# A two-layer graph kernel: output scaled by one VectorE instruction and added by GpSimd, probabilities' residual on VectorE, adjacency two graphs ahead, other orders at both ends

## The chip, the cores and the metric

The kernel runs on one core of a Trainium2 chip. The metric is the device time in microseconds of one execution, median over several. The engines named here are TensorE (PE, with its weight loads PEld), VectorE (DVE), ScalarE (ACT), GpSimd (POOL) and SyncE (SP), whose queue issues nearly all DMA transfers. They run side by side and wait for one another through semaphores only; each takes its own instructions strictly in order.

## The reference

`x` has 128 graphs of 128 nodes with 512 features, `adj` is one 128x128 matrix shared by all of them. Cut to what is computed:

```python
# layer 0
h = jnp.maximum(_layernorm(x), 0.0)
A = jnp.einsum('od,bdn->bon', adj, h)             # W1 = W2 = adj
C = A + b[None, :, None]
pre = A[:, :, None, :] + (C - A)[:, :, :, None]
x = x + jnp.max(jax.nn.relu(pre), axis=-1)
# layer 1
h = jnp.maximum(_layernorm(x), 0.0)
q, k, v = (h @ Wq + bq), (h @ Wk + bk), (h @ Wv + bv)    # 8 heads of 64
scores = einsum('bihd,bjhd->bhij', q, k) / 8 + mask(adj == 0)
x = x + einsum('bhij,bjhd->bihd', softmax(scores), v)
```

The kernel uses that layer 0 adds one number per node: the row's largest entry of `A` plus the bias, through a relu. A number that is the same for a whole row leaves the layer norm of layer 1 unchanged, so one normalised `h` serves both layers.

## The kernel before

One graph is one tile of 128 rows and 512 columns. Every matrix product is made of three fp16 products: each operand is split in a head (fp16 of the value) and a residual (fp16 of what the head leaves out), and head x head, head x residual and residual x head are summed in PSUM. So nearly every operand costs two instructions on ScalarE, VectorE or GpSimd: one for the head, one for the residual.

The work on the 128 graphs is a software pipeline written out by hand. Each engine has a function `slot(base, k)`, run for k = 0 to 127, and what it does in slot k belongs to graphs at fixed distances: x loaded 7 ahead (`LOAD_AHEAD`), statistics 6 ahead, normalised `h` 5 ahead, transposed `h` 5 ahead, adjacency product 4 ahead (`PREP_AHEAD`), its row maximum 3 ahead (`AMAX_AHEAD`); scores, softmax and value rows 5 behind, probabilities times values 6 behind, output 7 behind.

In slot k TensorE runs: `scores` of graph k-5 (24 matmuls), two `qk_chunk`s (12 matmuls each; a chunk is 128 columns of Wq or Wk for a group of four graphs, so eight chunks make a group), `adjacency` of graph k+4 (3 matmuls), `v_rows` of k-5 (12 matmuls), `probs_times_v` of k-6 (24 matmuls). ScalarE writes the heads, the two exponentials of each softmax (a head in fp16, a copy in fp32) and `x1`, the input plus layer 0's number. VectorE runs `adjacency_out` (the row maximum), `v_rest`, `softmax_shift` (`masked`, `row_max`, `shifted`), `attention_out` and the statistics. GpSimd computes the norm's scales and the residuals of `h`, of q/k (`qk_rest`) and of the probabilities (`probs_rest`), and adds the value bias to `x1` (`add_bv`). SyncE issues load, transpose of `h`, store and transpose of the probabilities, in that order in each slot.

PSUM has eight banks: two of `proj` for q/k chunks, `proj` bank 2 (`A_BANK`) for the adjacency product, `proj` bank 3 (`V_BANK`) for value rows, two of `sc` for scores, two of `o_ps` for the output. `adjacency(k)` waits until VectorE has taken the row maximum of graph k-1 out of `A_BANK` (`a_evac`), `v_rows` until `v_rest` of the graph before has emptied `V_BANK` (`v_evac`), `probs_times_v` until `attention_out` of the graph before has emptied `o_ps` (`y_done`).

Ahead of slot 0 stands a prologue. The weights come as fp32 and are scaled by a power of two that follows from their largest entry. For each of the four matrices VectorE finds the peak, TensorE brings it to all rows (`peak_to_rows`, o_ps<-ident,peak), VectorE makes the scale (`scales_of`), ScalarE writes the heads (`w_head`), VectorE the residuals (`w_rest`). The first four graphs are transposed on TensorE (`turn`) and copied out (`turn_out`), and their adjacency products go to four different banks (`FIRST_BANKS`). Slots 0 to 4 have orders of their own on GpSimd and ScalarE (`early_slot`). Behind slot 127 stands a tail of five graphs (`TAIL`), whose scores alternate between the banks of `sc` and of the q/k chunks.

Of the kernel before, what the change touches and what calls it, by code (L numbers as in the profile page):

```python
# [24 lines left out]
LOAD_AHEAD, MOMENTS_AHEAD, NORM_AHEAD, TURN_AHEAD, PREP_AHEAD, AMAX_AHEAD = 7, 6, 5, 5, 4, 3  # L25
ATTN_BEHIND, OUT_BEHIND, STORE_BEHIND = 5, 6, 7
V_BEHIND, V_OUT_BEHIND, Y_BEHIND, BV_BEHIND = 5, 6, 7, 4
HT_GROUPS = 3
DVE_RESTS = 3


def graph_layers(nc, x, adj, b0, wq, bq, wk, bk, wv, bv, out):
# [6 lines left out]
    with ExitStack() as ctx:  # L39
# [131 lines left out]
        def _(sp):  # L171
            def load(base, k):
                if in_range(base, k):

                    wait(sp, xc_done, base + k - RING + 1)
                    sp.dma_start(x_in[:, k % RING, :], x[base + k, :, :]).then_inc(x_loaded[k % RING], 16)

            def store(base, k):
                if in_range(base, k):
                    sp.wait_ge(y_done, base + k + 1)  # L180
                    sp.dma_start(out[base + k, :, :], y[:, k % 2, :]).then_inc(y_stored[k % 2], 16)
# [3 lines left out]
            for k in range(1, PREP_AHEAD):  # L185
                load(0, k)
# [25 lines left out]
            def slot(base, k):  # L212
                load(base, k + LOAD_AHEAD)
# [8 lines left out]
            for i in range(ATTN_BEHIND):  # L222
                transpose_probs(B, i - ATTN_BEHIND)
                if i != 2:
                    store(B, i - STORE_BEHIND - (i > 2))
            for k in range(-3, 0):
                store(B, k)
            for k in range(2):
                sp.wait_ge(y_stored[k], 16 * (B // 2))

        @block.gpsimd
        def _(pool):
# [48 lines left out]

            def qk_rest(base, k, u):
# [22 lines left out]
            pool.wait_ge(bias_loaded, 64)  # L305
            assert (NORM_AHEAD, MOMENTS_AHEAD) == (5, 6)

            def early_slot(base, k):
# [4 lines left out]
                rest(base, k + NORM_AHEAD)  # L313
                qk_rest(base, k, u + 1)
                norm_scales(base, k + MOMENTS_AHEAD)
                add_bv(base, k - BV_BEHIND)

            def slot(base, k):
# [4 lines left out]
                probs_rest(base, k - ATTN_BEHIND)  # L323
# [7 lines left out]
            for k in range(-BV_BEHIND, 0):  # L331
                add_bv(B, k)
            for graph in TAIL:
                probs_rest(*graph)

        @block.scalar
        def _(act):
            def normalise(base, k):

                if in_range(base, k):  # L340
# [496 lines left out]
```

## Time and profile before

| | |
|---|---|
| median of 3 runs | 1345.38 us (1343.56 to 1346.32) |
| the profiled execution, its own time | 1345.62 us |
| its span, first to last instruction | 1343.7 us |
| TensorE busy, share of the span | 1298.3 us, 97% |
| VectorE | 1076.1 us, 80% |
| ScalarE | 946.6 us, 70% |
| GpSimd | 1107.3 us, 82% |
| mean granted TensorE clock | 0.990 |

The span is 1.92 us shorter than the execution's own time. Busy shares are means over the whole span. The rows further down split the span in stretches: the start up to about 62 us, the steady part, and the tail behind the last slot, from 1292.68 us on.

### The profile page before, as it was taken

To read this page: it belongs to the slowest core of one execution; us is meant where nothing else is said; L and a number is where in the kernel's file an instruction comes from. 1 tells how busy PE (TensorE), PEld (TensorE's weight loads), DVE (VectorE), ACT (ScalarE), POOL (GpSimd) and SP (SyncE) were. 2 spreads that over 40 slices of the span, in tenths; PEclk is the share of its full clock that TensorE was granted. 3 is DMA by queue.
4 is the path that set the end of the run, shared out by engine and by line. 5 is a ranking of instruction groups with operands and counts; after the bars stand their busy time and mean duration, and the time that the engine had idled before them with its cause. 6 is when DMAs were issued, how large, how long until landed. Compare 5 with 4: busy or idle time off the path is not lost.

```text
span 1343.7 us, 30432 instructions
## 1 busy us (share of the span) xinstructions
PE 1298.3 (97%) x11177; PEld 681.4 (51%) x11177; DVE 1076.1 (80%) x2235; ACT 946.6 (70%) x1425; POOL 1107.3 (82%) x1160
## 2 busy tenths in 40 slices
PE   5899999999999999999999999999999999999984
PEld 2355555555555555555555555555555555555542
DVE  6678888888888878878878888888888888888677
ACT  5787777776776776776776777777777767767542
POOL 4589988988888888888888888888888888888662
PEclk9999999999999999999999999999999999999987
DMA  6345555555555655655555546545555555455424
GB/s 180 68 113 129 142 134 119 141 135 122 139 133 126 139 130 130 137 128 133 137 125 142 134 119 143 133 119 146 130 122 146 127 125 143 127 127 126 94 73 110
DMA packets 437316, 172.19 MB, mean 128 GB/s; under 512 B 402608, under 2 KB 402736, under 8 KB 437168
## 3 DMA queue, kind: packets, MB, share of 16 engines
q1 hardware_dynamic: 435824, 169.98, 53.0%
q8 instruction: 89, 1.46, 0.5%
q14 instruction: 59, 0.48, 0.1%
q10 hardware_dynamic: 1344, 0.27, 0.1%
HBM read 37.03 MB, written 33.55 MB: 53 GB/s over the span
## 4 chain that ended last, share of the span: by engine, by line
PE 94%; DVE 3%; ACT 1%; DMA 1%; issue 0%; SPq 0%; POOLq 0%; POOL 0%; ACTq 0%; DVEq 0%
PE proj L700 50%; PE proj L712 24%; PE sc L729 7%; PE o_ps L744 7%; PE proj L685 6%; DVE y L524 1%; DMA w_raw<-in_L_gnn_Wq 1%; DVE w L576 1%; DVE shifted L508 1%; DVE masked L501 0%; DVE row_max L505 0%; DMA out_x<-y 0%; ACT w L403 0%; POOLq L39 0%; ACT h L348 0%
## 5 line engine op out<-in xcount | busy, mean ns | idle before, releaser
L700 PE MATMUL proj<-hT,w 128*128 128x512 f16 x3072 | 688.6, 381 | 1.8 <-DVE w L576 1.1
L700 PEld LDWEIGHTS proj<-hT,w 128*128 128x128 f16 x3072 | 291.1, 98 | 350.5 <-issue 6.6
L712 PE MATMUL proj<-w,hT 128*128 128x512 f16 x1536 | 355.0, 381 | 9.9 <-DVE v L490 9.9
L360 ACT ACTIVATE qkT<-proj,bqk_up 128x512 f16<-128x512 f32 x256 | 173.8, 679 | 247.0 <-PE proj L700 246.9
L288 POOL TENSOR_TENSOR qkT<-qk,qkT 128x512 f16<-128x512 f32 x256 | 312.3, 1220 | 26.2 <-ACT qk L362 26.2
L295 POOL TENSOR_TENSOR probs<-probs 128x1024 f16<-128x1024 f32 x128 | 273.2, 2134 | 24.0 <-ACT probs L380 23.8
L712 PEld LDWEIGHTS proj<-w,hT 128*128 128x128 f16 x1536 | 150.4, 98 | 192.3 <-DVE v L490 10.6
L272 POOL TENSOR_TENSOR h<-h 128x512 f16<-128x512 f32 x125 | 236.5, 1892 | 12.8 <-ACT h L349 7.1
L490 DVE SCALAR_TENSOR_TENSOR v<-proj,v 128x512 f16<-128x512 f32 x128 | 88.5, 692 | 175.6 <-ACT v L368 175.6
L508 DVE TENSOR_TENSOR shifted<-masked,row_max 128x1024 f32<-128x1024 f32 x128 | 215.2, 1681 | 4.4
L524 DVE SCALAR_TENSOR_TENSOR y<-o_ps,out_scale,x 128x64 f32<-128x64 f32 x1024 | 208.3, 278 | 7.2 <-DMA out_x<-y 2.6
L501 DVE SCALAR_TENSOR_TENSOR masked<-sc,score_scale,mask 128x1024 f32<-128x1024 f32 x126 | 161.7, 1284 | 33.3 <-PE sc L729 33.1
L378 ACT ACTIVATE probs<-shifted 128x1024 f16<-128x1024 f32 x128 | 135.5, 1058 | 60.1 <-DVE shifted L508 60.0
L362 ACT ACTIVATE qk<-proj,bqk_up 128x512 f32<-128x512 f32 x256 | 173.9, 679 | 0.0
L280 POOL TENSOR_TENSOR x<-x,bv_rows 128x512 f32<-128x512 f32 x128 | 163.5, 1279 | 0.0
L505 DVE TENSOR_REDUCE row_max<-masked 128x8 f32<-128x1024 f32 x128 | 156.2, 1220 | 4.4
L380 ACT ACTIVATE probs<-shifted 128x1024 f32<-128x1024 f32 x128 | 133.4, 1042 | 0.0
L744 PEld LDWEIGHTS o_ps<-v,probsT 128*128 128x128 f16 x3072 | 112.1, 98 | 40.3 <-issue 11.1
L251 POOL TENSOR_TENSOR var_eps<-mean_var,eps 128x1 f32<-128x1 f32 x128 | 25.3, 198 | 128.6 <-DVE mean_var L477 128.6
L744 PE MATMUL o_ps<-v,probsT 128*128 128x65 f16 (+1 forms) x3072 | 115.8, 194 | 10.2 <-DVE y L524 10.2
L368 ACT ACTIVATE v<-proj 128x512 f16<-128x512 f32 x128 | 76.4, 597 | 61.8 <-PE proj L712 59.9
L348 ACT ACTIVATE h<-x_in,h_add,h_mul 128x512 f32<-128x512 f32 x128 | 103.4, 808 | 8.7 <-POOL h_add L261 6.2
(68 smaller groups left out, 1005.1 us busy)
## 6 DMA issues: line engine op xcount, KB each, us to landing
x_in<-in_x SPq DMA_DIRECT2D x128, 256.0 KB, 3.0
out_x<-y SPq DMA_DIRECT2D x128, 256.0 KB, 2.3
probsT<-probs SPq DMA_TRANSPOSE x128, 3.7
hT<-h SPq DMA_TRANSPOSE x124, 3.1
w_raw<-in_L_gnn_Wq SPq DMA_DIRECT2D x4, 256.0 KB, 7.6
w_raw<-in_L_gnn_Wk SPq DMA_DIRECT2D x1, 1024.0 KB, 9.3
w_raw<-in_L_gnn_Wv SPq DMA_DIRECT2D x1, 1024.0 KB, 11.3
bv_rows<-in_L_gnn_bv ACTq DMA_DIRECT2D x1, 256.0 KB, 6.9
```

The costliest lines, as they stand in the source:

```text
L272: pool.tensor_tensor(h16[:, k % 4, 1, :], h32[:, k % 2, :], h16[:, k % 4, 0, :], ALU.subtract).then_inc(h_rest_done, 1)
L280: pool.tensor_tensor(x1[:, k % RING, :], x1[:, k % RING, :], bv_rows[:, :], ALU.add).then_inc(x1_done, 1)
L288: pool.tensor_tensor(qk_place(k, u, 1), qk32[:, u % 2, :], qk_place(k, u, 0), ALU.subtract).then_inc(qk_rest_done, 1)
L295: pool.tensor_tensor(probs16[:, k % 2, 1, :, :], probs[:, :, :], probs16[:, k % 2, 0, :, :], ALU.subtract).then_inc(probs_rest_done, 1)
L360: nc.scalar.activation(qk_place(k, u, 0), place, ACT.Identity, scale=P_SCALE, bias=bias).then_inc(qk_head_done, 1)
L362: nc.scalar.activation(qk32[:, u % 2, :], place, ACT.Identity, scale=P_SCALE, bias=bias).then_inc(qk_evac, 1)
L501: nc.vector.scalar_tensor_tensor(masked[:, :, :], banks[:, :, :].rearrange("p t (h n) -> p (t h) n", n=P), score_scale[:, :], mask8[:, :]. ...
L508: nc.vector.tensor_tensor(shifted[:, :, :], masked[:, :, :], row_max[:, :].unsqueeze(2).to_broadcast([P, H, P]), ALU.subtract).then_inc(sh ...
L524: last = nc.vector.scalar_tensor_tensor(y[:, k % 2, cols], o_view[:, h // 4, h % 4, 0:HD], out_scale[:, h // 4, h % 4:h % 4 + 1], x1[:, k ...
L700: last = nc.tensor.matmul(proj[:, u % 2, :], w16[:, j, s, c, col * P:(col + 1) * P], hT[:, k // GROUP % HT_GROUPS, t, c, :, :].rearrange(" ...
L712: last = nc.tensor.matmul(proj[:, V_BANK, :], hT[:, (base + k) // GROUP % HT_GROUPS, s, c, k % GROUP, :], w16[:, 2, t, c, :], start=(c == ...
L744: last = nc.tensor.matmul(o_view[:, h // 4, h % 4, 0:w], probsT[:, k % 2, s, h % 2 * 4 + h // 2, :], v16[:, t, k % GROUP, h, 0:w], start=( ...
```

## The change

What it does, by parts:

- **Output.** `attention_out` had eight VectorE instructions of 64 columns, each scaling one head and adding `x1`. It now has one of 512 columns that scales all heads into a new buffer `attn`. GpSimd's new `finish` adds `x1` to it and writes `y`. `finish` and the store run eight slots behind, the scaling still seven. `probs_times_v` waits for `attn_done` in place of `y_done`.
- **Probabilities' residual.** `probs_rest` moves from GpSimd to VectorE in the 128 slots, at the end of the slot. In the tail it stays on GpSimd.
- **Adjacency.** It is computed two graphs ahead, not four (`PREP_AHEAD` 2, `AMAX_AHEAD` 1). Only graphs 0 and 1 stand in the prologue. Graphs 2 and 3 use the two banks of `sc`, graph 4 `A_BANK`, graph 5 `V_BANK`, and from 6 on `A_BANK`.
- **Start.** The first `h` residual, and the bias peaks, are done earlier on VectorE; the mask later; the row maxima of graphs 2 and 3 in slots 1 and 2. The `h` residual of graph 2 goes from VectorE to GpSimd (`DVE_RESTS` 2). VectorE copies out the turns of graphs 0, 1 and 3 and ScalarE that of graph 2, where it was graphs 0, 1 and 3 on ScalarE. `x_in` has ten buffers, and ten loads are issued ahead of slot 0.
- **Tail.** The value rows of the last graphs alternate between `A_BANK` and `V_BANK`, so each waits only for the graph two before it. TensorE, GpSimd and SyncE have other orders.

The diff, cut to its core:

```diff
-LOAD_AHEAD, MOMENTS_AHEAD, NORM_AHEAD, TURN_AHEAD, PREP_AHEAD, AMAX_AHEAD = 7, 6, 5, 5, 4, 3
-ATTN_BEHIND, OUT_BEHIND, STORE_BEHIND = 5, 6, 7
+LOAD_AHEAD, MOMENTS_AHEAD, NORM_AHEAD, TURN_AHEAD, PREP_AHEAD, AMAX_AHEAD = 7, 6, 5, 5, 2, 1
+ATTN_BEHIND, OUT_BEHIND, STORE_BEHIND = 5, 6, 8
-DVE_RESTS = 3
+DVE_RESTS = 2
...
+        def adjacency_bank(k):
+            return FIRST_BANKS[k] if k < len(FIRST_BANKS) else proj[:, A_BANK, :]
+        def v_bank(m):
+            return proj[:, A_BANK if m >= B - V_BEHIND and m % 2 == 0 else V_BANK, :]
...  GpSimd
+            def finish(base, k):
+                if in_range(base, k):
+                    m = base + k
+                    pool.wait_ge(attn_done, m + 1)
+                    pool.wait_ge(x1_done, m + 1)
+                    wait(pool, y_stored[m % Y_RING], 16 * (m // Y_RING))
+                    pool.tensor_tensor(y[:, m % Y_RING, :], attn[:, m % 2, :], x1[:, m % RING, :], ALU.add).then_inc(y_done, 1)
...  GpSimd, slot
                 norm_scales(base, k + MOMENTS_AHEAD)
-                probs_rest(base, k - ATTN_BEHIND)
+                finish(base, k - STORE_BEHIND)
                 qk_rest(base, k, u + 1)
...  GpSimd, behind the last slot
-            for k in range(-BV_BEHIND, 0):
-                add_bv(B, k)
-            for graph in TAIL:
-                probs_rest(*graph)
+            finish(B, -8)
+            finish(B, -7)
+            probs_rest(B, -5)
+            finish(B, -6)
+            add_bv(B, -4)
+            probs_rest(B, -4)
+            add_bv(B, -3)
+            probs_rest(B, -3)
+            add_bv(B, -2)
+            add_bv(B, -1)
+            probs_rest(B, -2)
+            finish(B, -5)
+            probs_rest(B, -1)
+            for k in range(-4, 0):
+                finish(B, k)
...  VectorE, attention_out
                     dve.wait_ge(out_scale_done, m + 1)
-                    dve.wait_ge(x1_done, m + 1)
-                    wait(dve, y_stored[k % 2], (m - k % 2) * 8)
-                    for h in range(H):
-                        cols = slice(h * HD, h * HD + HD)
-                        last = nc.vector.scalar_tensor_tensor(y[:, k % 2, cols], o_view[:, h // 4, h % 4, 0:HD],
-                                                              out_scale[:, h // 4, h % 4:h % 4 + 1],
-                                                              x1[:, k % RING, cols], ALU.mult, ALU.add)
-                    last.then_inc(y_done, 1)
+                    wait(dve, y_done, m - 1)
+                    nc.vector.tensor_tensor(attn[:, m % 2, :].rearrange("p (t h d) -> p t h d", t=2, d=HD),
+                                            o_view[:, :, :, 0:HD],
+                                            out_scale[:, :, :].unsqueeze(3).to_broadcast([P, 2, H // 2, HD]),
+                                            ALU.mult).then_inc(attn_done, 1)
...  VectorE, slot
-                if k > 0:
+                if k > 1:
                     stats_of(base, k + MOMENTS_AHEAD)
                     moments_wait(base, k + MOMENTS_AHEAD)
                     moments_of(base, k + MOMENTS_AHEAD)
+                probs_rest(base, k - ATTN_BEHIND)
...  TensorE, adjacency and v_rows
-                    wait(pe, a_evac, 1 if k == PREP_AHEAD else base + k)
+                    wait(pe, a_evac, base + k if k > len(FIRST_BANKS) else (0, 0, 0, 0, 1, 2, 5)[k])
-                    wait(pe, v_evac, base + k)
+                    wait(pe, v_evac, m if m < B - V_BEHIND + 1 else m - 1)
```

On TensorE at the start, from the first q/k chunk to slot 2 (`proj<-hT,w` are q/k chunks, `<-h,adjT` an adjacency product, `o_ps<-ident,peak` a weight peak brought to all rows), before:

```order
12 L700 MATMUL proj<-hT,w 128x512 x24
13 L685 MATMUL proj<-h,adjT 128x512 x3
14 L700 MATMUL proj<-hT,w 128x512 x12
15 L754 MATMUL o_ps<-ident,peak 128x128
16 L700 MATMUL proj<-hT,w 128x512 x12
17 L685 MATMUL proj<-h,adjT 128x512 x3
18 L700 MATMUL proj<-hT,w 128x512 x24
```

and now:

```order
10 L761 MATMUL proj<-hT,w 128x512 x24
11 L746 MATMUL sc<-h,adjT 128x512 x3
12 L761 MATMUL proj<-hT,w 128x512 x12
13 L822 MATMUL o_ps<-ident,peak 128x128
14 L761 MATMUL proj<-hT,w 128x512 x12
15 L746 MATMUL sc<-h,adjT 128x512 x3
16 L761 MATMUL proj<-hT,w 128x512 x24
```

The sequence of kinds is the same, but rows 13 and 17 of before are the products of graphs 4 and 5 in `A_BANK`, and rows 11 and 15 of now those of graphs 2 and 3, in two banks of their own.

On VectorE in a middle slot, from one `v_rest` to the next, before:

```order
710 L490 SCALAR_TENSOR_TENSOR v<-proj,v 128x8x64 [waits v_head_done]
711 L501 SCALAR_TENSOR_TENSOR masked<-sc,score_scale,mask 128x1024 [waits s_ready,shifted_done]
712 L505 TENSOR_REDUCE row_max<-masked 128x8 [waits masked_done]
713 L508 TENSOR_TENSOR shifted<-masked,row_max 128x1024 [waits probs_done,max_done]
714 L515 TENSOR_SCALAR scaled_sum<-o_ps,redo 128x8 [waits o_ready]
715 L518 RECIPROCAL out_scale<-scaled_sum 128x8 [waits sum_done]
716 L524 SCALAR_TENSOR_TENSOR y<-o_ps,out_scale,x 128x64 [waits y_stored0,x1_done,out_scale_done]
717 L524 SCALAR_TENSOR_TENSOR y<-o_ps,out_scale,x 128x64 x7
718 L467 BN_STATS stats<-x_in 128x6 [waits x_loaded5]
719 L477 BN_AGGR mean_var<-stats 128x2 [waits norm_done,bn_done]
720 L485 TENSOR_REDUCE a_max<-proj 128x1 [waits c_done,a_ready]
```

and now:

```order
713 L539 SCALAR_TENSOR_TENSOR v<-proj,v 128x8x64 [waits v_head_done]
714 L557 SCALAR_TENSOR_TENSOR masked<-sc,score_scale,mask 128x1024 [waits s_ready,shifted_done]
715 L561 TENSOR_REDUCE row_max<-masked 128x8 [waits masked_done]
716 L564 TENSOR_TENSOR shifted<-masked,row_max 128x1024 [waits probs_done,max_done]
717 L571 TENSOR_SCALAR scaled_sum<-o_ps,redo 128x8 [waits o_ready]
718 L574 RECIPROCAL out_scale<-scaled_sum 128x8 [waits sum_done]
719 L577 TENSOR_TENSOR attn<-o_ps,out_scale 128x512 [waits y_done,out_scale_done]
720 L516 BN_STATS stats<-x_in 128x6 [waits x_loaded9]
721 L526 BN_AGGR mean_var<-stats 128x2 [waits norm_done,bn_done]
722 L548 TENSOR_TENSOR probs<-probs 128x1024 [waits probs_done,probs_head_done]
723 L534 TENSOR_REDUCE a_max<-proj 128x1 [waits c_done,a_ready]
```

Eight `y` instructions have become one `attn`, and the probabilities' residual (`probs<-probs`) stands between the statistics and the row maximum, waiting for both exponentials.

On GpSimd at the program's end (`x<-x,bv_rows` is `add_bv`, `probs<-probs` the probabilities' residual), before:

```order
1150 L288 TENSOR_TENSOR qkT<-qk,qkT 128x512 [waits qk_head_done,qk_evac]
1151 L295 TENSOR_TENSOR probs<-probs 128x1024 [waits probs_done,probs_head_done]
1152 L288 TENSOR_TENSOR qkT<-qk,qkT 128x512 [waits qk_head_done,qk_evac]
1153 L280 TENSOR_TENSOR x<-x,bv_rows 128x512 [waits xc_done] x5
1154 L295 TENSOR_TENSOR probs<-probs 128x1024 [waits probs_done,probs_head_done] x5
```

and now:

```order
1157 L322 TENSOR_TENSOR probs<-probs 128x1024 [waits probs_done,probs_head_done]
1158 L298 TENSOR_TENSOR x<-x,bv_rows 128x512 [waits xc_done]
1159 L322 TENSOR_TENSOR probs<-probs 128x1024 [waits probs_done,probs_head_done]
1160 L298 TENSOR_TENSOR x<-x,bv_rows 128x512 [waits xc_done] x2
1161 L322 TENSOR_TENSOR probs<-probs 128x1024 [waits probs_done,probs_head_done]
1162 L307 TENSOR_TENSOR y<-attn,x 128x512 [waits y_stored1,x1_done,attn_done]
1163 L322 TENSOR_TENSOR probs<-probs 128x1024 [waits probs_done,probs_head_done]
1164 L307 TENSOR_TENSOR y<-attn,x 128x512 [waits y_stored0,x1_done,attn_done]
1165 L307 TENSOR_TENSOR y<-attn,x 128x512 [waits y_stored1,x1_done,attn_done]
```

The value bias additions now stand between the five residuals, not ahead of them, and the last additions of the output (`y<-attn,x`), new on this engine, stand around the last residual and behind it.

## Rows read from the trace of the kernel before

**Rows 1.** Windows: start, length, busy us (and instructions) by engine, clock, DMA share, GB/s.
```profile
20.00:40.00 20.00, 13.87 (x56) 5.91 (x57) 14.91 (x29) 13.90 (x24) 8.95 (x17) 0.91 0.31 54
40.00:60.00 20.00, 19.09 (x81) 8.21 (x79) 8.93 (x19) 13.85 (x23) 13.02 (x19) 0.92 0.32 69
...
800.00:1000.00 200.00, 200.00 (x1738) 105.23 (x1737) 163.69 (x338) 145.35 (x221) 173.63 (x181) 1.00 0.56 132
```

**Rows 2.** Groups by line, whole span: busy us, mean ns | idle before, releaser.
```profile
L524 DVE SCALAR_TENSOR_TENSOR y<-o_ps,out_scale,x 128x64 f32<-128x64 f32 x1024 | 208.3, 278 | 7.2 <-DMA out_x<-y 2.6
L508 DVE TENSOR_TENSOR shifted<-masked,row_max 128x1024 f32<-128x1024 f32 x128 | 215.2, 1681 | 4.4
L490 DVE SCALAR_TENSOR_TENSOR v<-proj,v 128x512 f16<-128x512 f32 x128 | 88.5, 692 | 175.6 <-ACT v L368 175.6
L295 POOL TENSOR_TENSOR probs<-probs 128x1024 f16<-128x1024 f32 x128 | 273.2, 2134 | 24.0 <-ACT probs L380 23.8
L272 POOL TENSOR_TENSOR h<-h 128x512 f16<-128x512 f32 x125 | 236.5, 1892 | 12.8 <-ACT h L349 7.1
L288 POOL TENSOR_TENSOR qkT<-qk,qkT 128x512 f16<-128x512 f32 x256 | 312.3, 1220 | 26.2 <-ACT qk L362 26.2
L380 ACT ACTIVATE probs<-shifted 128x1024 f32<-128x1024 f32 x128 | 133.4, 1042 | 0.0
```

**Rows 3.** TensorE's timeline at the start: start us, length us, what, [idle before <-releaser].
```profile
20.04 5.34 PE L700 MATMUL proj<-hT,w 128*128 128x512 f16 x24 [1.08 <-DVE w L576]
28.26 0.82 PE L685 MATMUL proj<-h,adjT 128*128 128x512 f16 x3 [2.89 <-POOL h L272]
28.92 4.44 PE L700 MATMUL proj<-hT,w 128*128 128x512 f16 x12
33.20 0.38 PE L754 MATMUL o_ps<-ident,peak 128*128 128x128 f32 x2
...
39.38 1.03 PE L685 MATMUL proj<-h,adjT 128*128 128x512 f16 x3 [3.21 <-DVE a_max L485]
...
61.27 0.81 PE L685 MATMUL proj<-h,adjT 128*128 128x512 f16 x3 [1.47 <-DVE a_max L485]
62.02 0.84 PE L729 MATMUL sc<-qkT 64*128 64x128 f16 x24
62.79 5.35 PE L700 MATMUL proj<-hT,w 128*128 128x512 f16 x24
67.98 0.81 PE L685 MATMUL proj<-h,adjT 128*128 128x512 f16 x3
68.63 2.75 PE L712 MATMUL proj<-w,hT 128*128 128x512 f16 x12
71.31 0.84 PE L729 MATMUL sc<-qkT 64*128 64x128 f16 x24
```

**Rows 4.** VectorE's timeline: the residuals of Wk.
```profile
35.31 3.13 DVE L576 SCALAR_TENSOR_TENSOR w<-w_raw,up,w 128x512 f16<-128x512 f32 x4 [0.45 <-ACT w L403]
```

**Rows 5.** TensorE's timeline in the tail.
```profile
1292.68 0.84 PE L729 MATMUL sc<-qkT 64*128 64x128 f16 x24
...
1300.95 5.30 PE L712 MATMUL proj<-w,hT 128*128 128x512 f16 x12 [3.96 <-DVE v L490]
...
1337.60 1.47 PE L744 MATMUL o_ps<-v,probsT 128*128 128x65 f16 x24 [4.86 <-DVE y L524]
```

**Rows 6.** VectorE's timeline in the tail.
```profile
1312.25 1.22 DVE L508 TENSOR_TENSOR shifted<-masked,row_max 128x1024 f32<-128x1024 f32 x1
...
1316.56 2.31 DVE L508 TENSOR_TENSOR shifted<-masked,row_max 128x1024 f32<-128x1024 f32 x1
...
1323.98 1.22 DVE L508 TENSOR_TENSOR shifted<-masked,row_max 128x1024 f32<-128x1024 f32 x1
...
1339.61 1.63 DVE L524 SCALAR_TENSOR_TENSOR y<-o_ps,out_scale,x 128x64 f32<-128x64 f32 x8
```

**Rows 7.** DMA issues: median us from issue to landing.
```profile
probsT<-probs SPq DMA_TRANSPOSE x128, 3.7
```

More of the change, by code:

```diff
@@ L180, in store @@
                     sp.wait_ge(y_done, base + k + 1)
[L181 removed]
+                    sp.dma_start(out[base + k, :, :], y[:, (base + k) % Y_RING, :]).then_inc(y_stored[(base + k) % Y_RING], 16)
             load(0, 0)
             sp.dma_start(adj_sb[:, :], adj).then_inc(adj_loaded, 16)
[L185 removed]
+            for k in range(1, GROUP):
                 load(0, k)
@@ L189, in _ @@
             sp.dma_start(w_raw[:, 1, :, :], wk.rearrange("(c p) n -> p c n", p=P)).then_inc(w_loaded[1], 16)
-            for k in range(PREP_AHEAD, LOAD_AHEAD):
+            for k in range(GROUP, 2 * GROUP):
                 load(0, k)
             sp.dma_start(w_raw[:, 2, :, :], wv.rearrange("(c p) n -> p c n", p=P)).then_inc(w_loaded[2], 16)
+            for k in range(2 * GROUP, X_RING):
+                load(0, k)
             def transpose(base, k):
@@ L221, in _ @@
                 slot(0, k)
[L222 to L226, printed above, removed]
+            store(B, -8)
+            store(B, -7)
+            transpose_probs(B, -5)
+            store(B, -6)
+            transpose_probs(B, -4)
+            transpose_probs(B, -3)
+            transpose_probs(B, -2)
+            store(B, -5)
+            transpose_probs(B, -1)
+            for k in range(-4, 0):
                 store(B, k)
-            for k in range(2):
-                sp.wait_ge(y_stored[k], 16 * (B // 2))
+            for k in range(Y_RING):
+                sp.wait_ge(y_stored[k], 16 * (B // Y_RING))
         @block.gpsimd
@@ L805, in _ @@
                 slot(0, k)
-            for i, (base, k) in enumerate(TAIL):
-                if i == 1:
-                    pe.wait_ge(qk_evac, 2 * B)
-                if i > 1:
-                    pe.wait_ge(masked_done, base + k - 1)
-                scores(base, k, TAIL_BANKS[i % 2])
-                v_rows(base, k)
-                if i == 1 or i == 3:
-                    probs_times_v(B, i // 2 - OUT_BEHIND)
+            scores(B, -5)
+            v_rows(B, -5)
+            pe.wait_ge(qk_evac, 2 * B)
+            scores(B, -4, TAIL_BANKS[1])
+            v_rows(B, -4)
+            probs_times_v(B, -6)
+            pe.wait_ge(masked_done, B - 4)
+            scores(B, -3, TAIL_BANKS[0])
+            v_rows(B, -3)
+            pe.wait_ge(masked_done, B - 3)
+            scores(B, -2, TAIL_BANKS[1])
+            probs_times_v(B, -5)
+            v_rows(B, -2)
+            pe.wait_ge(masked_done, B - 2)
+            scores(B, -1, TAIL_BANKS[0])
+            v_rows(B, -1)
             for k in range(-4, 0):
```

164 lines of the change are left out of this document (93 added, 71 removed).

## The prediction

> **What bounds the kernel now.** I read the windows first. In the steady part TensorE is busy 200.00 of 200 us at full clock, VectorE 163.69, ScalarE 145.35, GpSimd 173.63 [rows 1]: TensorE sets the time there, and the others only have to stay under its period. That period comes from two starts of `scores`, of graph 1 at 71.31 and of graph 123 at 1292.68 [rows 3, 5]: 122 slots in 1221.4 us. An adjacency product takes 0.65 (67.98 to 68.63 [rows 3]), and the last four slots had none, so a slot is (1221.4 + 2.6)/122 = 10.03 us. Per slot, VectorE then works 8.21, ScalarE 7.29 and GpSimd 8.71.
>
> What isn't bound by TensorE's work stands at both ends, so next I read TensorE's timeline there. From its first chunk at 20.04 to the second `scores` at 71.31 it runs twelve chunks (six pairs of 5.19, from 62.79 to 67.98), six adjacency products, two peaks at 0.22, one `scores` at 0.77 and value rows at 2.68 [rows 3]: 31.1 + 3.9 + 0.4 + 0.8 + 2.7 = 38.9 us of work in 51.3. So 12.4 us are lost. The reader is to see three idle times in the brackets: 2.89 ahead of 28.26 (graph 4's adjacency waits for GpSimd's residual of `h`), 3.21 ahead of 39.38 and 1.47 ahead of 61.27 (the adjacency waits for a row maximum that stands behind weight work on VectorE) [rows 3]. The clock adds (0.09 + 0.08) x 20 = 3.4 us: the windows show 0.91 and 0.92 [rows 1], and 12 matmuls at 28.92 took 4.44 where 24 take 5.34 [rows 3], about the 1.2 GHz level, behind the idle time. The rest is smaller waits.
>
> The tail runs from 1292.68 to the span's end at 1343.7: 51.0 us. TensorE waits in it for VectorE: 3.96 for `v_rest` ahead of 1300.95, after which 12 matmuls took 5.30 at the lower clock, and 4.86 for `y` ahead of 1337.60 [rows 5].
>
> **The middle: cost of the change 0.** TensorE's list per slot is the same. VectorE loses eight `y` instructions, 208.3/128 = 1.63 us per graph [rows 2]. It gains `attn`: the trace has no such instruction; bounds are one 64-column `y` (0.28) and all eight (1.63), the nearest row `v_rest`, 512 columns from PSUM, 0.69 [rows 2], which I take. It gains the probabilities' residual: nearest is `shifted`, VectorE, 1024 columns from SBUF, 1.22 at best [rows 6], 1.68 on average, 2.31 in the tail [rows 2, 6]. Sum: 8.21 - 1.63 + 0.69 + 1.22 to 2.31 = 8.5 to 9.6, under 10.03. GpSimd loses 2.13 and gains `finish`, priced like `qk_rest` at 1.22 [rows 2]: 8.71 - 2.13 + 1.22 = 7.8.
>
> `shifted` shows a wait inside its duration: 1.22 at 1312.25, 2.31 at 1316.56 [rows 6]. GpSimd's `h` residual takes 1.89 where `qk_rest`, of the same size, takes 1.22, while `v_rest`, with one input in PSUM, stays at 0.69 [rows 2]. I read it as VectorE with two SBUF inputs and GpSimd excluding one another for a whole instruction. The Trainium skill (SBUF — State Buffer, "Who interferes with whom") has the same rule: a VectorE instruction with two SBUF inputs contends with a GpSimd instruction that reads SBUF, and the second to issue blocks fully. By that rule this change makes the collisions worse, with two such VectorE instructions per graph instead of one; the trace agrees on `shifted`.
>
> The new residual also waits for both exponentials. The loop on VectorE is then `masked` 1.3, `row_max` 1.25, `shifted` 1.25, exponentials 2.1 (twice 1.04 [rows 2]), residual 1.25, row maximum 0.7, `v_rest` 0.75: 8.6, with scaling and statistics, 2.0, hidden under the exponentials. `shifted` waits 1.68 - 1.22 = 0.46 for GpSimd on average; with the same for the residual the loop is 9.5. I take it as covered. Cover gone, each 0.1 us over 10.03 costs 12 us. The store moves a slot back and stands ahead of the probabilities' transpose in SyncE's queue; that waits for `finish`, near 10.8 us into the slot, and lands 3.7 later [rows 7], at 4.5 of the next slot, while `probs_times_v` wants it at 9.2. Also 0.
>
> **The start: gain 10.1.** The first chunk stays bound by Wq's peak, scale, heads and residuals; work moved within it gives about 0.1. Then the adjacency of graphs 2 and 3 finds its `h` ready and a bank of its own: the idle 2.89 and 3.21, and with them the 3.4 of clock, go. What is late next is Wk. Its peak reaches TensorE behind the third chunk, at 20.0 + 5.2 + 0.65 + 2.6 = 28.4 (before: 33.20 [rows 3]). From there to the last residual took 35.31 + 3.13 - 33.20 = 5.2 us [rows 3, 4], so 33.6; TensorE wants the first of the four at 28.4 + 0.2 + 2.6 + 0.65 = 31.9 and the last 1.95 later, at 33.8. That just fits. Next is ScalarE: from 20 to 60 us it works 13.90 + 13.85 = 27.75 [rows 1], and must do the same by about 51, in 31 us. It fits with queueing; I leave 1.0 us of stalls, between 0 and 4. The transposes of graphs 4 to 7 (needed near 44 us) come through GpSimd's queue, which I find done some 1.5 us ahead.
>
> So 12.4 - 1.0 + 0.1 = 11.5 saved up to the second `scores`. But two adjacency products that ran ahead of the first chunk, while TensorE had time, now come in full slots: 2 x 0.65 = 1.3 lost. 11.5 - 1.3 = 10.2; with rounding, 10.1. If the clock stays at the lower level at the first chunk, behind a TensorE gap of 2 us, 1.7 is lost again.
>
> The Trainium skill (TensorE: Matmul & The Clock Gate, "What's actually happening") says that activity releases the throttle and idleness brings it back. By that the 3.4 us can only go if the idle times do; the trace agrees, with both falls behind the two long gaps.
>
> **The tail: gain 8.0.** VectorE's chain binds. Before, its last `shifted` ends at 1325.20, 32.5 after the tail began, and the end comes 18.5 later [rows 5, 6]. From 1313.47, the end of one `shifted`, to the next at 1316.56 `v_rest`, `masked` and `row_max` take 3.09 [rows 6]; with `shifted` 4.31 per graph. Now: the first ends 4.7 in (0.84 of scores, 3.09 - 0.6, 1.22 [rows 5, 6] and handoffs), four more are 17.2, three output scalings at 0.22 + 0.20 + 0.69 + handoff = 1.15 are 3.5, and waits for GpSimd's 2.13 residuals I put at 2.8 in all (one of them was 2.31 - 1.22 = 1.09): 28.2. The waits for `v_rest` (3.96) and their clock fall away, since value rows need only the graph two before. Saved: 4.3. Then exponentials 2.2, residual 2.13, transpose 3.7, product 1.47, scaling 1.15, `finish` 1.27, and 2.46 from the last `y` (1341.24) to the end: 14.4 against 18.5 [rows 2, 5 to 7]. Saved: 4.1. The last `finish` but one waits for a store that SyncE issues behind the last transpose; by my times it comes 1.0 us early. 8.4; I take 8.0, between 3 and 10.
>
> **Sum.** 1345.62 - 10.1 - 8.0 = 1327.5 us. The profiled execution stands 0.24 over the median of the runs, which changes nothing.
>
> **The rivals.**
> *The residual makes VectorE the bound* (slower). Speaks for it: `shifted` already waits up to 1.09, and the new one may wait as much or, behind an addition of GpSimd's, 1.22. It decides when both waits together pass 10.03 - 8.6 = 1.4 us per graph. At 1.7 (0.85 each) the middle grows by 0.3 x 122 = 37: 1364. Against it: 0.46 is the mean with GpSimd at 8.71, and its load falls. If the two never overlap, GpSimd's 7.8 plus 2 x 1.22 gives 10.2 at worst, or 9.6 where 7.8 already holds the waits for `shifted`: near the edge, so 9 in 100. (The Trainium skill's exclusive lock, same page, is this case; it would put the time by which of the two sums is right.)
> *ScalarE or the transposes take over at the start*: 4 us of new stalls, and 1.7 of clock, 1332 to 1334. For: 27.75 us of work in 31. Against: TensorE's waits there never were for ScalarE alone. 12 in 100.
> *The tail only shifts*: the last transpose, and the stores behind it, come as late as before, gain 3: 1332.5. 8 in 100.
> *No change that can be measured*: both ends re-form their waits elsewhere; 1343 to 1348. It needs both of the two above in full. 5 in 100.
>
> **How the numbers follow.** The forecast case holds 66 in 100, with 1323 to 1331. The range 1320 to 1340 adds the two partial cases and leaves out the slower rival, no change, and the forecast's edges, under 2 in 10. A measurement can tell about 0.2%, 2.7 us, from no change: faster 0.86, same 0.05, slower 0.09.
>
> **What the changed profile would show.** Middle: TensorE still 200 of 200, period 10.03, VectorE 8.9 to 9.5 per slot, `probs<-probs` on VectorE between 1.22 and 2.4, GpSimd under 9. If TensorE idles there, waiting for VectorE, the forecast is wrong at once. Start: no idle of 2 us from 20 on, clock 1.00 after 20, second `scores` near 60. Tail: begins near 1282, lasts 43, no wait for `v_rest` ahead of value rows. Wrong would be an idle time ahead of the fifth chunk (Wk's residuals), the ninth (transposes) or the eleventh (ScalarE).

## The result, and the profile after

The changed kernel takes 1557.82 us (median of 4 runs, 1556.41 to 1558.26), the kernel before 1344.47 beside it: ratio 1.158 (1.156 to 1.160, a 95% interval, as behind every ratio below), 213 us slower. The forecast, 1327.5, has the wrong sign. The profiled execution took 1556.41, with a span of 1554.6.

The windows of the changed kernel, in the stretches of [rows 1] (columns as there):

```profile
20.00:40.00 20.00, 19.03 (x80) 8.18 (x81) 17.49 (x34) 14.68 (x24) 14.35 (x24) 0.89 0.16 35
40.00:60.00 20.00, 20.00 (x116) 9.41 (x114) 13.09 (x24) 17.86 (x32) 14.69 (x22) 1.00 0.41 93
800.00:1000.00 200.00, 176.25 (x1465) 89.95 (x1466) 143.01 (x183) 119.52 (x185) 132.43 (x151) 0.97 0.46 108
```

The start filled up as forecast. In the steady part every engine works less than before, TensorE 176.25 of 200 (at a granted clock of 0.97, so part of that is slower matmuls), and none is full: VectorE 143.01, GpSimd 132.43. So no engine has become the bound by its load. When all of them have idle time, something goes round between them. The chain that ended last (the page's part 4) says who takes part:

```profile
DVE 45%; POOL 24%; issue 17%; ACT 7%; PE 4%; POOLq 1%; ACTq 1%; DMA 1%; SPq 0%; DVEq 0%
```

TensorE has 4% of it. The waits of the changed kernel (who waits <- for whom: us in total, times, longest) name the links:

```profile
POOL var_eps L269 <- DVE mean_var L526: 364.9, 121, 5.2
DVE v L539 <- ACT v L415: 339.4, 123, 3.2
ACT probs L425 <- DVE shifted L564: 293.4, 124, 4.4
ACT x L445 <- POOL y L307: 281.9, 114, 2.7
...
PE o_ps L812 <- DVE attn L577: 173.3, 117, 5.2
```

One of them is new in kind: ScalarE's write of `x1` (`x<-x_in`, L445) waits 114 times for GpSimd's `y`. In the kernel before this write waits for nothing (0.2 us idle in all). Here is one period on the three engines (timeline: start, length, what, [idle before <-releaser]); first ScalarE:

```profile
816.98 0.72 ACT L445 ACTIVATE x<-x_in,c_col 128x512 f32<-128x512 f32 x1 [2.43 <-POOL y L307]
817.61 0.58 ACT L415 ACTIVATE v<-proj 128x512 f16<-128x512 f32 x1
```

VectorE:

```profile
818.22 0.69 DVE L539 SCALAR_TENSOR_TENSOR v<-proj,v 128x512 f16<-128x512 f32 x1 [2.90 <-ACT v L415]
818.83 1.28 DVE L557 SCALAR_TENSOR_TENSOR masked<-sc,score_scale,mask 128x1024 f32<-128x1024 f32 x1
820.14 1.22 DVE L561 TENSOR_REDUCE row_max<-masked 128x8 f32<-128x1024 f32 x1
821.39 1.96 DVE L564 TENSOR_TENSOR shifted<-masked,row_max 128x1024 f32<-128x1024 f32 x1
...
824.37 0.68 DVE L516 BATCH_NORM_STATS2 stats<-x_in 128x6 f32<-128x512 f32 x1
825.09 0.18 DVE L526 BATCH_NORM_AGGREGATE mean_var<-stats 128x2 f32<-128x6 f32 x1
825.49 1.23 DVE L548 TENSOR_TENSOR probs<-probs 128x1024 f16<-128x1024 f32 x1 [0.22 <-ACT probs L427]
```

GpSimd, the end of one slot and the beginning of the same work a period later:

```profile
813.62 1.51 POOL L271 TENSOR_TENSOR inv_std<-var_eps,minus_half 128x1 f32<-128x1 f32 x1
815.21 0.20 POOL L276 TENSOR_TENSOR h_mul<-inv_std,plus_minus 128x2 f32<-128x2 f32 x1
815.48 0.19 POOL L279 TENSOR_TENSOR h_add<-mean_var,h_mul 128x1 f32<-128x1 f32 x1
815.62 1.26 POOL L307 TENSOR_TENSOR y<-attn,x 128x512 f32<-128x512 f32 x1
...
825.35 0.19 POOL L269 TENSOR_TENSOR var_eps<-mean_var,eps 128x1 f32<-128x1 f32 x1 [3.08 <-DVE mean_var L526]
825.62 1.51 POOL L271 TENSOR_TENSOR inv_std<-var_eps,minus_half 128x1 f32<-128x1 f32 x1
```

Read from start to start: `inv_std` 813.62, `h_mul` 815.21, `y` 815.62, ScalarE's `x` 816.98, its `v` 817.61, VectorE's `v` 818.22, `masked` 818.83, `row_max` 820.14, `shifted` 821.39, `stats` 824.37, `mean_var` 825.09, `var_eps` 825.35, and `inv_std` again at 825.62. The loop is closed, and it takes 12.00 us, where TensorE needs 10.03.

Why these wait for one another stands in three places of the code. ScalarE writes `x1` of graph k into one of eight buffers (RING = 8), at the end of slot k, once graph k-8 has been read out of it:

```python
wait(act, y_done, m - RING + 1)     # add_c, ScalarE, last in slot k
...
finish(base, k - STORE_BEHIND)      # GpSimd, slot k: reads x1 of graph k-8, behind norm_scales
...
v_head(base, k - V_OUT_BEHIND)      # ScalarE, first in slot k+1: behind add_c in the same queue
```

Before, the reader was VectorE's `attention_out`, seven slots behind: graph k-8 had been read a whole slot earlier. Now it is `finish`, eight slots behind, in the very slot in which ScalarE wants the buffer, and behind `norm_scales`, which waits for the statistics at the end of VectorE's slot. ScalarE, waiting, holds `v_head` of the next slot; VectorE's slot begins with what that delivers, and ends with the statistics. The first `x` that waits so stands at 94.82.

### The profile page after: what moved, and what is told of

Read it like the earlier page. It is cut to its first block, busy times and chain, and to the rows that moved or that the text cites. A ratio compares the mean times of both kernels' runs of the same rounds, so it can differ in the third digit from the quotient of the medians.

```text
span 1554.6 us, 29792 instructions
## 1 busy us (share of the span) xinstructions
PE 1356.8 (87%) x11177; PEld 689.7 (44%) x11177; DVE 1129.2 (73%) x1463; ACT 931.7 (60%) x1423; POOL 1022.6 (66%) x1166
## 4 chain that ended last, share of the span: by engine, by line
DVE 45%; POOL 24%; issue 17%; ACT 7%; PE 4%; POOLq 1%; ACTq 1%; DMA 1%; SPq 0%; DVEq 0%
DVE shifted L564 15%; POOL inv_std L271 11%; DVE masked L557 10%; DVE row_max L561 10%; POOL y L307 9%; DVE stats L516 5%; ACT v L415 4%; PE proj L761 2%; DVE out_scale L574 2%; POOL h_mul L276 2%; POOL var_eps L269 1%; DVE mean_var L526 1%; DVE scaled_sum L571 1%; PE proj L778 1%; POOL h_add L279 1%
## 5 line engine op out<-in xcount | busy, mean ns | idle before, releaser
L761 PE MATMUL proj<-hT,w 128*128 128x512 f16 x3072 | 719.8, 393 | 1.7 <-DVE hT L681 1.5
L761 PEld LDWEIGHTS proj<-hT,w 128*128 128x128 f16 x3072 | 298.7, 101 | 376.0 <-issue 50.8
L315 POOL TENSOR_TENSOR qkT<-qk,qkT 128x512 f16<-128x512 f32 x256 | 300.1, 1172 | 28.1 <-ACT qk L409 28.1
L445 ACT ACTIVATE x<-x_in,c_col 128x512 f32<-128x512 f32 x128 | 92.4, 722 | 282.0 <-POOL y L307 281.9
L564 DVE TENSOR_TENSOR shifted<-masked,row_max 128x1024 f32<-128x1024 f32 x128 | 245.6, 1919 | 4.4
L290 POOL TENSOR_TENSOR h<-h 128x512 f16<-128x512 f32 x126 | 146.2, 1161 | 95.1 <-ACT h L395 83.6
L812 PEld LDWEIGHTS o_ps<-v,probsT 128*128 128x128 f16 x3072 | 105.5, 98 | 232.5 <-issue 227.5
L271 POOL TENSOR_TENSOR inv_std<-var_eps,minus_half 128x1 f32<-128x1 f32 x128 | 179.1, 1399 | 10.0
L548 DVE TENSOR_TENSOR probs<-probs 128x1024 f16<-128x1024 f32 x123 | 151.5, 1232 | 37.6 <-ACT probs L427 37.5
L307 POOL TENSOR_TENSOR y<-attn,x 128x512 f32<-128x512 f32 x128 | 164.8, 1288 | 8.7 <-DVE attn L577 6.6
```

What stands on the lines that cost most here:

```text
L271: pool.tensor_tensor(inv_std[:, r, :], var_eps[:, r, :], minus_half[:, :], ALU.pow).then_inc(norm_step, 1)
L307: pool.tensor_tensor(y[:, m % Y_RING, :], attn[:, m % 2, :], x1[:, m % RING, :], ALU.add).then_inc(y_done, 1)
L315: pool.tensor_tensor(qk_place(k, u, 1), qk32[:, u % 2, :], qk_place(k, u, 0), ALU.subtract).then_inc(qk_rest_done, 1)
L564: nc.vector.tensor_tensor(shifted[:, :, :], masked[:, :, :], row_max[:, :].unsqueeze(2).to_broadcast([P, H, P]), ALU.subtract).then_inc(sh ...
L761: last = nc.tensor.matmul(proj[:, u % 2, :], w16[:, j, s, c, col * P:(col + 1) * P], hT[:, k // GROUP % HT_GROUPS, t, c, :, :].rearrange(" ...
L812: last = nc.tensor.matmul(o_view[:, h // 4, h % 4, 0:w], probsT[:, k % 2, s, h % 2 * 4 + h // 2, :], v16[:, t, k % GROUP, h, 0:w], start=( ...
```

## The experiments

The loop is theory A. Its rival, theory B, is the one of the prediction: the residual on VectorE and its exclusion with GpSimd make the slot longer. Theory A can be opened at the buffer or at the reader.

**One more buffer for `x1`,** nothing else:

```diff
-        x1 = sb("x1", [P, RING, D])
+        x1 = sb("x1", [P, X1_RING, D])        # X1_RING = 9; its index is m % X1_RING everywhere
...
-                    wait(act, y_done, m - RING + 1)
+                    wait(act, y_done, m - X1_RING + 1)
```

> The changed kernel with nine buffers for x1 instead of eight; all else as changed. Theory A (ring): ScalarE's writing of x1 for graph k waits until GpSimd has finished graph k-8, which GpSimd does in the same slot behind the norm's scales, which wait for VectorE's statistics at the slot's end; so one slot's end starts the next slot's value head, and the slot is 12.0 us. With nine buffers the wait is for graph k-9, finished a slot earlier: slot 10.03, the middle again bound by TensorE, span 1554.6 - 122 x 1.86 = 1327, time 1329 (1325 to 1335). Theory B (exclusion): the two VectorE instructions with two SBUF inputs and GpSimd's work take turns, and this makes the slot; nothing here touches them, so 1500 to 1560.

Measured: 1328.74 (1327.87 to 1329.0), ratio 0.987 (0.985 to 0.990). The window of the steady part, then the cost of `inv_std`, `shifted` and the residual on VectorE from the groups by line (busy, mean ns | idle before):

```profile
800.00:1000.00 200.00, 200.00 (x1739) 105.23 (x1737) 171.81 (x219) 145.25 (x221) 165.03 (x181) 1.00 0.59 132
```

```profile
L565 DVE TENSOR_TENSOR shifted<-masked,row_max 128x1024 f32<-128x1024 f32 x128 | 218.4, 1706 | 4.4
L272 POOL TENSOR_TENSOR inv_std<-var_eps,minus_half 128x1 f32<-128x1 f32 x128 | 178.5, 1394 | 10.0
L549 DVE TENSOR_TENSOR probs<-probs 128x1024 f16<-128x1024 f32 x123 | 152.0, 1236 | 37.7 <-ACT probs L428 37.7
L446 ACT ACTIVATE x<-x_in,c_col 128x512 f32<-128x512 f32 x128 | 91.6, 716 | 0.2
```

229 us come back with one buffer. TensorE is full again, `x` waits for nothing, and all durations on which theory B rests are still there: `inv_std` 1.39, `shifted` 1.71, residual 1.24 on average. The 1500 to 1560 of theory B is ruled out.

**The reader first, eight buffers.** GpSimd's `finish` moves ahead of `rest` and `norm_scales` in its slot; nothing else.

```diff
             def slot(base, k):
                 u = 2 * (k % GROUP)
+                finish(base, k - STORE_BEHIND)
                 rest(base, k + NORM_AHEAD)
                 qk_rest(base, k, u)
                 norm_scales(base, k + MOMENTS_AHEAD)
-                finish(base, k - STORE_BEHIND)
```

> The changed kernel with eight buffers for x1, but GpSimd finishes graph k-8 first in slot k, ahead of the residual of h and of the norm's scales. Theory A: the addition no longer waits for the statistics of the same slot; the cycle is open, slot 10.03, time 1329 (1325 to 1335). Theory B: the same instructions and the same exclusion, 1500 to 1560.

Measured: 1328.39 (1327.56 to 1328.76), ratio 0.987 (0.984 to 0.990). In its timelines GpSimd's `y` starts 6.5 us before the `x` that needs it, and `x` has no idle time before it:

```profile
814.74 1.27 POOL L307 TENSOR_TENSOR y<-attn,x 128x512 f32<-128x512 f32 x1
```

```profile
821.28 0.72 ACT L445 ACTIVATE x<-x_in,c_col 128x512 f32<-128x512 f32 x1
```

The same distance in slots, the same work, the same buffers: only the place in the slot differs.

**The residual back on GpSimd, behind `finish`, eight buffers.** This separates what the exclusion adds to the loop from the loop itself.

```diff
                 finish(base, k - STORE_BEHIND)
+                probs_rest(base, k - ATTN_BEHIND)     # GpSimd
...
-                probs_rest(base, k - ATTN_BEHIND)     # VectorE
```

> The changed kernel with the probabilities' residual back on GpSimd, behind the finishing addition; x1 has eight buffers. Theory A: the cycle keeps all its links and loses only the time for which the norm's second scale instruction waits for VectorE (1.51 instead of 0.55, so 0.96), and one wait of the shifted instruction may change by up to 1: slot 11.0 to 12.0, time 1430 to 1560. Theory B: the second colliding instruction is gone from VectorE, slot back to 10.03, 1330 to 1350.

Measured, one run: 1460.68. The loop stands, shorter. Waits, then two `masked` in VectorE's timeline:

```profile
ACT x L446 <- POOL y L307: 172.5, 114, 1.8
```

```profile
811.57 1.28 DVE L558 SCALAR_TENSOR_TENSOR masked<-sc,score_scale,mask 128x1024 f32<-128x1024 f32 x1
...
822.79 1.27 DVE L558 SCALAR_TENSOR_TENSOR masked<-sc,score_scale,mask 128x1024 f32<-128x1024 f32 x1
```

The period is 11.22. `inv_std` is back at 0.55 (552 ns on average), 0.96 less than the 1.51 in the loop of the changed kernel; `shifted` in this period took 2.15 in place of 1.96, 0.19 more. 12.00 - 0.96 + 0.19 = 11.23. So the residual on VectorE lengthens the loop, and doesn't make it; theory B wanted 1330 to 1350 here.

**`finish` two instructions later,** behind the second `qk_rest` and `add_bv`; eight buffers.

```diff
-                finish(base, k - STORE_BEHIND)
                 qk_rest(base, k, u + 1)
                 add_bv(base, k - BV_BEHIND)
+                finish(base, k - STORE_BEHIND)
```

> The changed kernel with the finishing addition put two instructions later in GpSimd's slot, behind the second q/k residual (1.13) and the value bias addition (1.22). Theory A: the cycle grows by their 2.35 us, slot 14.4, time 1557 + 119 x 2.35 = 1837 (1780 to 1850). Theory B: the same work in another order, 1520 to 1600.

Measured, one run: 1842.52. The wait grows as the theory says (281.9 before):

```profile
ACT x L445 <- POOL y L307: 570.5, 120, 5.1
```

(1842.52 - 1557.82)/122 = 2.33 us per slot. In the timeline `qk_rest` and `add_bv` put 2.34 us into the loop (`qk_rest` starts at 810.27, `y` at 812.61), and from one `inv_std` to the next it is 14.33 us (808.27 to 822.60) in place of 12.00. In this kernel's list of waits nobody waits for the results of these two instructions; they cost their full length because the reader stands behind them.

**Nine buffers and the residual on GpSimd.** With the loop open, what is moving the residual worth?

> Nine buffers for x1, and the probabilities' residual back on GpSimd behind the finishing addition: what moving the residual buys once the cycle is open. With the residual there GpSimd was busy 178.1 of 200 us at a slot of 11.0 in the kernel with eight buffers, 9.8 per slot. Theory A: the cycle is gone, GpSimd's 9.8 plus its waits for VectorE's statistics lie about at TensorE's 10.03: slot 10.0 to 10.4, 1330 to 1375. Theory B (exclusion by the residual on VectorE costs the time): under 1329.

Measured: 1345.76 (1344.34 to 1346.42, 10 runs), ratio 1.000 (0.999 to 1.002). Its window:

```profile
800.00:1000.00 200.00, 199.66 (x1724) 102.09 (x1723) 160.31 (x199) 141.29 (x217) 195.30 (x199) 1.00 0.57 131
```

GpSimd, given `finish` and keeping the residual, works 195.30 of 200, and it has 55% of the chain that ended last. From the second `scores` (62.35) to that of graph 123 (1301.30) go 1238.95 us, 16.2 more than 122 slots at TensorE's pace. So the two moves belong together: the residual must leave if `finish` comes, and is then worth 17.0 us (1345.76 - 1328.74). The residual on VectorE without `finish` was not tried.

**The new ends alone, with the middle of before:** eight `y` on VectorE, no `finish`, the store seven slots behind, the residual on GpSimd.

```diff
-ATTN_BEHIND, OUT_BEHIND, STORE_BEHIND = 5, 6, 8
+ATTN_BEHIND, OUT_BEHIND, STORE_BEHIND = 5, 6, 7
...
-                finish(base, k - STORE_BEHIND)
+                probs_rest(base, k - ATTN_BEHIND)
...
-                    wait(pe, attn_done, m)
+                    wait(pe, y_done, m)
```

> The changed start and tail with the middle of before: eight output instructions on VectorE that add x1 themselves, no finishing addition, the residual on GpSimd, store seven behind, eight x1 buffers. Theory A: no link from GpSimd's addition to ScalarE, so slot 10.03; the start as in the kernel with nine buffers; in the tail seven scalings of 2.08 instead of 1.15, less one addition of 1.3: 2 to 5 us longer than there. 1331 to 1334. Rival: the gains of the ends hang on the new output, 1338 to 1345.

Measured: 1332.45 (1330.87 to 1333.23), ratio 0.991 (0.989 to 0.993). Its tail, from the `scores` of graph 123 at 1282.27 to the span's end at 1328.7, takes 46.4. With the new middle and nine buffers it is 42.75 (1283.35 to 1326.1). So of the 8.3 us by which the tail shrank from 51.0, 4.6 come of the tail's other changes (orders and value banks) and 3.7 of the shorter scaling and the addition on GpSimd. The medians differ by the same 3.7 (1332.45 - 1328.74), and in the steady part TensorE is full in both, as it was before: shorter output work on VectorE buys nothing there, only in the tail.

**One bank for the value rows in the tail,** nine buffers:

```diff
-            return proj[:, A_BANK if m >= B - V_BEHIND and m % 2 == 0 else V_BANK, :]
+            return proj[:, V_BANK, :]
...
-                    wait(pe, v_evac, m if m < B - V_BEHIND + 1 else m - 1)
+                    wait(pe, v_evac, m)
```

> Nine buffers for x1, and all value rows of the tail through one bank again, with the wait for the graph before. If the waits for VectorE's value residual were part of what bound the tail of before, 2 to 4 us longer than with two banks: 1331 to 1333. If only VectorE's own work bounds it: 1329.

Measured: 1329.45 (1328.08 to 1330.66), ratio 0.989 (0.987 to 0.991): no difference from 1328.74 that can be told. TensorE's timeline has the waits for `v_rest` again:

```profile
1290.41 2.76 PE L779 MATMUL proj<-w,hT 128*128 128x512 f16 x12 [2.19 <-DVE v L540]
...
1296.03 2.76 PE L779 MATMUL proj<-w,hT 128*128 128x512 f16 x12 [1.35 <-DVE v L540]
...
1301.78 2.76 PE L779 MATMUL proj<-w,hT 128*128 128x512 f16 x12 [1.37 <-DVE v L540]
```

With 2.94 ahead of a fourth, that is 7.85 us of TensorE's idle time, and the tail, 1283.90 to 1326.6, is 42.7, as with two banks. VectorE's chain sets this tail, and these idle times cost it nothing. All four times the 12 matmuls behind the wait took 2.76 us, the upper clock.

**`x1` written a slot later,** eight buffers: ScalarE writes `x1` of graph k-1 in slot k, behind the exponentials.

```diff
+                if k > ATTN_BEHIND:
+                    add_c(base, k - 1)
                 qk_out(base, k, u + 1)
-                add_c(base, k)
...
             v_head(B, -V_OUT_BEHIND)
+            add_c(B, -1)
```

> The changed kernel with eight x1 buffers and GpSimd's order unchanged; ScalarE writes x1 of graph k-1 in slot k, behind the exponentials, where it wrote x1 of graph k at the end of slot k. GpSimd's finish still stands behind the statistics. Theory A: the cycle closes only because ScalarE's in-order queue keeps the next slot's value head behind the waiting x1 instruction; with the buffer's reader now a slot in the past there is no wait, slot 10.03, 1329 (1326 to 1333). Theory B (exclusion by the residual): 1500 to 1560.

Measured: 1329.31 (1328.46 to 1329.78), ratio 0.988 (0.986 to 0.989). In this kernel the last graph's `x1` was made from another graph's input (the instructions and waits are the same); a second version reads its own:

> As the kernel before it, which wrote x1 of graph k-1 in slot k on ScalarE, but the last graph's x1 now reads that graph's own x buffer (there it read another graph's, with the same instructions and waits). Theory A: 1329 again (1327 to 1331). Theory B (exclusion): 1500 to 1560.

Measured: 1328.57 (1328.15 to 1329.83), ratio 0.988 (0.986 to 0.990). So the loop opens at the writer as well as at the reader or the buffer.

**The adjacency products of graphs 2 and 3 ahead of the first chunk,** nine buffers; graph 3's takes the other `o_ps` bank. It gives back the 1.3 us that the prediction booked as lost.

```diff
             turn(2)
+            adjacency(0, 2)
             turn(3)
+            adjacency(0, 3)
...
-                adjacency(base, k + PREP_AHEAD)
+                if k > 1:
+                    adjacency(base, k + PREP_AHEAD)
```

> Nine buffers for x1, and the adjacency products of graphs 2 and 3 ahead of the first chunk, as in the kernel before (graph 3's in an output bank). Two terms of the forecast: 2 x 0.65 us come back into TensorE's idle time, and the gap ahead of the first chunk shrinks, so the clock may stay at the upper level (the first 24 matmuls took 7.03, 5.34 at the upper level). Both: 1329 - 1.3 - 1.7 = 1326. Clock unchanged: 1327.5.

Measured: 1326.86 (1326.45 to 1326.95), ratio 0.987 (0.985 to 0.989), between the two forecasts. The clock stayed up (36 matmuls in 7.93, granted clock 1.00), but TensorE now waits 0.69 and 0.70 for Wk's residuals. Last, `finish` first and these early products together, with eight buffers:

> The changed kernel with GpSimd's finish first in its slot (eight x1 buffers) and the adjacency products of graphs 2 and 3 ahead of the first chunk: the two separate remedies together, no memory added. By the nine-buffer kernel with the same early products: 1326.9. If the products moved 1.3 us into idle time and the clock holds: 1326 to 1327.5; if the clock falls at the first chunk: 1328.

Measured: 1326.45 (1326.28 to 1326.92, 4 runs), ratio 0.986 (0.984 to 0.987): the fastest here, 19 us under the kernel before. TensorE's timeline at its start:

```profile
19.36 7.93 PE L763 MATMUL proj<-hT,w 128*128 128x512 f16 x36 [1.25 <-DVE hT L681]
27.12 0.39 PE L824 MATMUL o_ps<-ident,peak 128*128 128x128 f32 x2
27.35 2.75 PE L763 MATMUL proj<-hT,w 128*128 128x512 f16 x12
30.81 2.10 PE L763 MATMUL proj<-hT,w 128*128 128x512 f16 x9 [0.71 <-DVE w L629]
33.61 3.41 PE L763 MATMUL proj<-hT,w 128*128 128x512 f16 x15 [0.69 <-DVE w L629]
```

Its second `scores` comes at 58.78. Against 60.38 with nine buffers that is 1.60 less: 1.30 for two products and 1.69 for the clock of the first chunk (below), less 1.40 for Wk's residuals, which TensorE now reaches before they are done (0.71 and 0.69). That makes 1.59; an idle time of 0.21 at the same place with nine buffers, and later starts of some hundredths, are left out of it.

## Why the prediction was wrong

**The step that failed is "The middle: cost of the change 0."** By the two `scores` of the trace after, its 122 slots took 1511.88 - 62.02 = 1449.86 us, 11.88 each, where 10.03 makes 1222.7 with the last slots' missing adjacency: +227. Everything else adds up to -16.3: the second `scores` at 62.02 for 71.31 (-9.3), the two adjacency products that now stand in full slots (+1.3), and a tail of 42.7 for 51.0 (-8.3). 1343.7 + 227.2 - 16.3 = 1554.6, the span.

**What was missing in that step.** The prediction moved each instruction, priced it, and followed the store into SyncE's queue. It did not list whose buffers the moved reader frees. `x1` has as many buffers as slots between ScalarE's write and GpSimd's read. The one loop that it added up, VectorE with ScalarE's exponentials (8.6 to 9.5), leaves GpSimd out, and the rival *The residual makes VectorE the bound* asked whether loads and mutual waits fit under 10.03. They do; a loop over three in-order queues is something else. The prediction's own check ("If TensorE idles there, waiting for VectorE, the forecast is wrong at once") does catch the profile after, for another cause than the one that it had in mind. With one buffer more the cost of the middle is 0, as forecast.

**The steps of the middle that stood,** read with nine buffers: TensorE 200 of 200; `attn` 0.69, the value chosen between 0.28 and 1.63; the residual on VectorE 1.24, at the low end of 1.22 to 2.31; VectorE 171.81/19.94 = 8.62 us per slot (200/10.03 = 19.94 slots), inside the sum's 8.5 to 9.6 and under the 8.9 to 9.5 of the list of signs; GpSimd 165.03/19.94 = 8.28, where 7.8 stood. The largest term missing in the 7.8 is `inv_std`, 1.39 in place of 0.55, 0.84 more; the residual of `h`, 1.22 in place of 1.89, gives 0.67 back. The prediction let the residual wait for GpSimd, and it is one of GpSimd's smallest instructions that waits for the residual. In the lines above `inv_std` starts at 825.62, 0.13 behind the residual's start, and ends at 827.13, 0.41 after the residual's end. The Trainium skill (SBUF — State Buffer, "Who interferes with whom") says that the order of issue decides who blocks; the trace agrees, 1.51 in place of 0.55, and it also shows that the blocked one is a 128x1 instruction that stood in a loop.

**The start.** Forecast: second `scores` near 60, measured 62.02 in the changed kernel and 60.38 with nine buffers. None of the idle times of 2 us is left after 20 us. The risk named, the lower clock at the first chunk (1.7), came true: 24 matmuls took 7.21 where 5.34 is the upper level, 1.87 more, and 7.03 with nine buffers, 1.69 more. That 60.38 is still near 60 is in part luck: the first chunk starts 0.73 earlier than before (19.31 for 20.04), where 0.1 was booked, and the stalls booked with 1.0 are one idle time of 0.21.

**The tail.** Forecast 43, measured 42.7. The last `shifted` in VectorE's timeline of the changed kernel:

```profile
1538.70 1.35 DVE L564 TENSOR_TENSOR shifted<-masked,row_max 128x1024 f32<-128x1024 f32 x1
```

It ends at 1540.05, 28.2 after the tail began, as the sum said, and 14.6 more follow (14.4 forecast). But the reason given for the first 4.3 us, that the waits for `v_rest` and their clock fall away, holds only in part. The waits alone cost nothing: the kernel with one value bank has them. What did cost time before was the first of them together with the lower clock behind it (12 matmuls in 5.30 [rows 5]). VectorE then idled for the product that follows these matmuls, and near the end it idled once more, for a store (VectorE's timeline, kernel before):

```profile
1307.05 0.23 DVE L515 TENSOR_SCALAR scaled_sum<-o_ps,redo 128x8 f32<-128x8 f32 x1 [2.44 <-PE o_ps L744]
...
1335.83 1.63 DVE L524 SCALAR_TENSOR_TENSOR y<-o_ps,out_scale,x 128x64 f32<-128x64 f32 x8 [2.58 <-DMA out_x<-y]
```

In the kernel with the ends alone the first of these is gone, and 0.31 is left of the second. Its last `shifted` ends 29.7 into the tail (32.5 before), and 16.7 more follow (18.5): 2.8 and 1.8, the 4.6 us of the tail's other changes. That is read from the traces; no run changes these parts one at a time. The rest, 29.7 to 28.2 and 16.7 to 14.6, comes with the shorter scaling and the addition on GpSimd.

**Were the loop not there,** the sum would have been right to 1.2 us: 1328.74 or 1328.39 for 1327.5, with the luck at the start. That doesn't save it: the change that was timed has the loop.

## What to carry to other kernels

When the reader of a ring buffer moves to another engine or a slot back, write down which read the writer waits for, where in its slot that read stands, and what stands behind the writer in its own queue; if the distance is as long as the ring, follow the chain backwards until it ends or comes round. A loop that closes once per slot costs, in every slot, its length less the period that the busiest engine needs (12.00 less 10.03 here), however light each engine's load. It shows as a profile in which no engine is full, with a chain that ended last that passes TensorE by. The order inside a slot can cure it: here one instruction moved to the front was worth as much as a ninth buffer.

## What the hardware showed

**TensorE's clock at the first chunk isn't settled by the idle time ahead of it.** Two kernels with the same idle time, first that with nine buffers, then that with the ends alone:

```profile
19.31 7.03 PE L762 MATMUL proj<-hT,w 128*128 128x512 f16 x24 [1.90 <-DVE hT L682]
```

```profile
19.32 5.34 PE L756 MATMUL proj<-hT,w 128*128 128x512 f16 x24 [1.90 <-DVE hT L677]
```

In the 2 us from 19 and the 2 us from 21 the granted clock was 0.63 and 0.52 in the first and 1.00 in the second. Of the eight other profiles with this start, with 1.48 to 2.20 of idle time, none stayed up: 24 matmuls took 7.03 to 8.02. The two with adjacency products in between, with 1.25 and 1.28, did (36 matmuls in 7.93). Each is one execution, and what decides between 7.03 and 5.34 stays open.

**The granted clock of a profile can miss a slow stretch.** In two of these eight, both with 2.20 of idle time, 24 matmuls took 7.94 and 8.02, while the clock in the rows reads 1.00 from 20 to 40 us. There the duration of the matmuls is the surer sign.

**A tiny GpSimd instruction can wait longer than it works** for one VectorE instruction with two inputs in SBUF: `inv_std`, 128x1, took 0.55 us on average where the residual ran on GpSimd, 1.39 to 1.40 where it ran on VectorE, in every kernel of the two kinds.
